# Pair attention in a small transformer kernel: every fourth partition, four chunks of 512 tokens, eight unrolled blocks, keys read in place

## The reference

```
x = x + _L1_attn_ref(_layernorm(x, axis=-1), Wq, Wk, Wv)

b, s, d = x.shape                       # 64, 32, 128; H = 16
Q = (x @ Wq.T).reshape(H, b, s, 8)      # K, V alike
scores = jnp.einsum('hbqd,hbkd->hbqk', Q, K)
atten = jax.nn.softmax(scores, axis=-1)
out = jnp.einsum('hbqk,hbkd->hbqd', atten, V).reshape(b, s, -1)
y = out + x
mu = jnp.mean(y, axis=(1, 2), keepdims=True)
var = jnp.var(y, axis=(1, 2), keepdims=True)
return (y - mu) / jnp.sqrt(var + 1e-5)
```

## Time and profile before

| | us |
|---|---|
| median of three runs | 3089.42 |
| lowest, highest | 3085.68, 3090.41 |
| the profiled execution, its own time | 3081.74 |
| the span of its trace | 3080.0 |

### The profile page before, as it was taken

The page is one execution under the profiler, slowest core; times in us unless marked ns, Lnnn a source line. Parts: engine busy times, 40 slices in busy tenths (PEclk is TensorE's granted clock), DMA queues, the critical chain, the costliest instruction groups (busy, mean ns, idle before and its releaser), DMA issues. The chain is left out here.

```text
span 3080.0 us, 35217 instructions
## 1 busy us (share of the span) xinstructions
PE 2488.2 (81%) x11867; PEld 1402.0 (46%) x11875; DVE 2267.4 (74%) x3046; ACT 1868.9 (61%) x2572; POOL 902.2 (29%) x498
## 2 busy tenths in 40 slices
PE   6699999998899999999999999954366641435998
PEld 3366666663344444444444444322355521423665
DVE  4487777754999999999999999855899921534443
ACT  4365555545888888888888889842455520013443
POOL 1021111111444444444444444300200031102665
PEclk9899999999999999999999999975667775557999
DMA  1000000001000000000000000000011013010000
GB/s 53 11 25 15 18 18 14 14 8 69 1 0 35 1 35 0 34 0 35 0 34 0 35 0 0 0 11 16 10 35 34 21 36 49 5 29 33 16 16 14
DMA packets 17732, 60.16 MB, mean 20 GB/s; under 512 B 1520, under 2 KB 10032, under 8 KB 15664
## 3 DMA queue, kind: packets, MB, share of 16 engines
q1 hardware_dynamic: 17584, 58.29, 6.2%
HBM read 53.04 MB, written 5.24 MB: 19 GB/s over the span
## 5 line engine op out<-in xcount | busy, mean ns | idle before, releaser
L251 PE MATMUL a_ps<-a_x,a_w 128*128 128x512 f32 x1536 | 695.6, 598 | 24.7 <-DVE a_kf L599 12.4
L251 PEld LDWEIGHTS a_ps<-a_x,a_w 128*128 128x128 f32 x1536 | 291.5, 191 | 404.3 <-issue 367.8
L774 POOL TENSOR_TENSOR a_den<-a_qf,a_ksum 128x1024 f32<-128x1024 f32 x128 | 271.2, 2119 | 510.2 <-DVE a_qf L592 473.5
L777 POOL TENSOR_TENSOR a_num<-a_qf,a_kvsum 128x1024 f32<-128x1024 f32 x128 | 295.0, 2304 | 186.1 <-DVE a_kvsum L617 186.0
L2137 DVE TENSOR_REDUCE x_rn<-x_sqk 128x8 f32<-128x512 f32 x256 | 174.3, 681 | 104.8 <-ACT x_sqk L2061 100.6
L2061 ACT ACTIVATE x_sqk<-x_b_k 128x512 f32<-128x512 f32 x256 | 153.1, 598 | 155.8 <-PE x_b_k L1973 149.3
L262 PE MATMUL a_ps<-a_att,a_w 128*128 128x512 f32 x480 | 215.8, 592 | 0.0
L592 DVE SCALAR_TENSOR_TENSOR a_qf<-a_eq,a_qf 128x1024 f32<-128x1024 f32 x128 | 195.4, 1526 | 1.7
L1954 POOL TENSOR_TENSOR x_kn<-x_craw,x_w 128x256 f32<-128x256 f32 x64 | 47.1, 736 | 509.7 <-DVE x_craw L2126 488.1
L445 ACT ACTIVATE a_den<-a_den,consts 128x1024 f32<-128x1024 f32 x128 | 147.0, 1149 | 57.3 <-POOL a_den L774 57.3
L599 DVE SCALAR_TENSOR_TENSOR a_kf<-a_ek,a_ps 128x1024 f32<-128x1024 f32 x128 | 155.5, 1215 | 27.8 <-ACT a_ps L441 23.1
(11 more groups left out here) (417 smaller groups left out, 5480.3 us busy)
## 6 DMA issues: line engine op xcount, KB each, us to landing
a_w<-layers SPq DMA_DIRECT2D x8, 2577.0 KB, 9.2
x_craw<-ctx SPq DMA_DIRECT2D x32, 256.0 KB, 2.6
y_cx<-ctx_t SPq DMA_DIRECT2D x16, 512.0 KB, 3.2
m_w<-experts SPq DMA_DIRECT2D x8, 608.0 KB, 3.8
x_w<-xattn_w SPq DMA_DIRECT2D x1, 2048.0 KB, 7.3
x_all<-x_t SPq DMA_DIRECT2D x1, 1024.0 KB, 4.9
t_scratch<-t_tmp SPq DMA_DIRECT2D x1, 1024.0 KB, 3.9
t_q<-t_scratch SPq DMA_DIRECT2D x4, 256.0 KB
```

The source lines that it names most:

```text
L251: last = nc.tensor.matmul(bank(tile, j), col(par, part * HK + u * P, P), x[:, t0:t0 + BANK], start=True, stop=True)
L774: nc.gpsimd.tensor_tensor(by_batch(den[:, b, :]), by_batch(qf[:, b, :]), bcast(ksum[:, b, :], S), ALU.mult).then_inc(d_ready, 1)
L777: nc.gpsimd.tensor_tensor(by_batch(num[:, b, :]), by_batch(qf[:, b, :]), bcast(kvsum[:, b, :], S), ALU.mult).then_inc(n_ready, 1)
```

## The change

The stage becomes one block of code without barriers inside.

- The layout by heads uses partitions 32g, 32g + 4, ..., 32g + 28 (`ROW_STEP = 4`) instead of 32g to 32g + 7. The zeros between stay, so products read all 32 rows.
- The feature norm is written out in the stage, with ScalarE squaring. q and v are kept by ScalarE, k by VectorE, each in quarters of 512 tokens; a quarter is stored and spread by heads by itself, in an order written out by hand.
- There are 8 blocks of half the size, unrolled, and scores, staged q, turned v and turned probabilities have two buffers. TensorE reads the keys of a pair from `by_head[1]` directly (16 runs of two neighbouring numbers, 2 KB apart), so GpSimd stages only q.
- After every two blocks the outputs of 128 tokens of each quarter (a chunk of 512 tokens) go to DRAM and come back, and the batch norm of the chunk is done among the later blocks. VectorE sums over a batch first, and TensorE then averages 16 sums instead of 512 tokens.

```
@@ -1306,9 +1306,14 @@
 GROUPS = 4
 GTOK = TOK // GROUPS
 PAIR_ROWS = 2 * HEADS
-BLOCKS = 4
+
+
+BLOCKS = 8
 BPAIRS = GTOK // 2 // BLOCKS
 BCOL = BPAIRS * PAIR_ROWS
+ROW_STEP = 4
+CHUNKS = 4
+CTOK = TOK // CHUNKS
...
-            by_head = [sbi(n + "8", [P, HEADS, GTOK]) for n in "qkv"]
-            staged = [sbi(n + "s", [P, BCOL]) for n in "qkv"]
...
-                        for i in range(3):
-                            sp.wait_ge(kept, 2 * i + 2)
-                            sp.dma_start(scratch[i], qkv_t[i][:, :]).then_inc(stored, 16)
-                            sp.wait_ge(stored, 16 * (i + 1))
-                            if i == 0:
-                                sp.wait_ge(cleared, 3)
-                            for g in range(GROUPS):
-                                sp.dma_start(by_head[i][32 * g:32 * g + DH, :, :],
-                                             scratch[i].rearrange("(j c) t -> c j t", c=DH)[:, :, g * GTOK:(g + 1) * GTOK]
-                                             ).then_inc(spread, 16)
...
-                    def _(pool):
-                        for t in by_head:
-                            nc.gpsimd.memset(t[:, :, :], 0.0).then_inc(cleared, 1)
...
-                                r = slice(32 * g, 32 * g + DH)
-                                last = nc.tensor.matmul(psum_s[32 * g:32 * g + 32, c], staged[0][r, c], staged[1][r, c],
-                                                        start=True, stop=True)
-                            last.then_inc(scored, 1)
...
-                        scores(0, True)
-                        with pe.Fori(0, BLOCKS - 1) as i:
-                            scores(i + 1)
-                            outputs(i)
-                        outputs(BLOCKS - 1)
...
-                        with pool.Fori(0, BLOCKS) as i:
-                            pool.wait_ge(s_used, i + 1)
-                            nc.gpsimd.tensor_copy(rows_of(staged[0]), heads_of(by_head[0], i)).then_inc(q_staged, 1)
-                            nc.gpsimd.tensor_copy(rows_of(staged[1]), heads_of(by_head[1], i)).then_inc(k_staged, 1)
...
-                        sp.wait_ge(o_free, BLOCKS + 1)
-                        for g in range(GROUPS):
-                            sp.dma_start(scratch[3].rearrange("(j c) t -> c j t", c=DH)[:, :, g * GTOK:(g + 1) * GTOK],
-                                         o8[32 * g:32 * g + DH, :, :]).then_inc(o_stored, 16)
-                        sp.wait_ge(o_stored, 16 * GROUPS)
-                        sp.dma_start(o_t[:, :], scratch[3]).then_inc(gathered, 16)
-                        sp.wait_ge(gathered, 16)
...
+        q_st = sb("qs", [P, 2, BCOL])
+        v_st = sb("vs", [P, BCOL])
+        v_rows = sb("v_rows", [P, 2, BCOL])
+        prob = sb("prob", [P, BCOL])
+        prob_t = sb("prob_t", [P, 2, BCOL])
+        red = sb("red", [P, BPAIRS])
+        sums = sb("sums", [P, 4, TOK // S])
+        o8, o_t, square = by_head[0], tmp, q_t
...
+        def scores_of(i):
+            return ps[:, i % 2 * BCOL:(i % 2 + 1) * BCOL]
+
+        out_ps = ps[:, 4 * BANK:4 * BANK + BCOL]
+        mean_ps, var_ps = bank(6), bank(7)
...
+        def chunk(ap, c):
+
+            return ap[:, :].rearrange("p (g t) -> p g t", g=GROUPS)[:, :, c * P:(c + 1) * P]
+
+        def packed(ap, c):
+
+            return ap[:, of(c)].rearrange("p (g t) -> p g t", g=GROUPS)
+
+        def rows_in(g):
+            return slice(32 * g, 32 * (g + 1), ROW_STEP)
+
+        def in_scratch(i, g, first, last):
+
+            return scratch[i].rearrange("(j c) t -> c j t", c=DH)[:, :, g * GTOK + first:g * GTOK + last]
...
+                def store(i, p):
+                    sp.wait_ge(kept[i], p + 1)
+                    sp.dma_start(scratch[i][:, of(p)], qkv_t[i][:, of(p)]).then_inc(stored[i][p], 16)
+
+                def by_heads(i, p):
+                    sp.wait_ge(stored[i][p], 16)
+                    sp.wait_ge(cleared, i + 1)
+                    sp.dma_start(by_head[i][rows_in(p), :, :], in_scratch(i, p, 0, GTOK)).then_inc(spread[i], 16)
...
+                store(0, 0)
+                store(0, 1)
+                store(1, 0)
+                by_heads(0, 0)
+                store(0, 2)
+                store(1, 1)
+                by_heads(0, 1)
+                by_heads(1, 0)
+                store(0, 3)
+                store(1, 2)
+                by_heads(0, 2)
+                by_heads(1, 1)
+                store(1, 3)
+                by_heads(0, 3)
+                store(2, 0)
+                by_heads(1, 2)
+                store(2, 1)
+                by_heads(1, 3)
+                store(2, 2)
+                by_heads(2, 0)
+                store(2, 3)
+                for p in range(1, 4):
+                    by_heads(2, p)
...
+                def store_output(first, last):
+                    for g in range(GROUPS):
+                        sp.dma_start(in_scratch(3, g, first, last), o8[rows_in(g), :, first:last]).then_inc(o_stored, 16)
+
+                stores = 0
+                for c in range(CHUNKS):
+                    if c < CHUNKS - 1:
+                        sp.wait_ge(o_kept, 2 * c + 2)
+                        store_output(c * P, (c + 1) * P)
+                        stores += GROUPS
+                    else:
...
+                            sp.wait_ge(o_kept, 2 * c + 1 + h)
+                            store_output(c * P + h * (P // 2), c * P + (h + 1) * (P // 2))
+                            stores += GROUPS
+                    sp.wait_ge(o_stored, 16 * stores)
+                    sp.dma_start(packed(o_t, c), chunk(scratch[3], c)).then_inc(o_loaded[c], 16)
...
+            def _(pool):
+                for t in by_head:
+                    nc.gpsimd.memset(t[:, :, :], 0.0).then_inc(cleared, 1)
+                for i in range(BLOCKS):
+                    if i == 0:
+                        pool.wait_ge(spread[0], 16 * GROUPS)
+                    wait_past(pool, scored, i - 1)
+                    nc.gpsimd.tensor_copy(rows_of(q_st[:, i % 2, :]), heads_of(by_head[0], i)).then_inc(q_staged, 1)
...
+                def scores(i):
+                    pe.wait_ge(q_staged, i + 1)
+                    if i == 0:
+                        pe.wait_ge(spread[1], 16 * GROUPS)
+                    wait_past(pe, shifted, i - 1)
+                    out = scores_of(i)
+                    for g, n in turns():
+                        c = slice(n * PAIR_ROWS, (n + 1) * PAIR_ROWS)
+                        r = slice(32 * g, 32 * g + 32)
+                        t = 2 * (i * BPAIRS + n)
+                        last = nc.tensor.matmul(out[r, c], q_st[r, i % 2, c], by_head[1][r, :, t:t + 2], start=True, stop=True)
+                    last.then_inc(scored, 1)
+
+                def outputs(i):
+                    pe.wait_ge(v_turned, i + 1)
+                    pe.wait_ge(p_turned, i + 1)
+                    wait_past(pe, o_kept, i)
+                    for g, n in turns():
+                        c = slice(n * PAIR_ROWS, (n + 1) * PAIR_ROWS)
+                        r = slice(32 * g, 32 * g + 32)
+                        last = nc.tensor.matmul(out_ps[r, c], v_rows[r, i % 2, c], prob_t[r, i % 2, c], start=True, stop=True)
+                    last.then_inc(attended, 1)
...
+                def batch_mean(c):
+                    pe.wait_ge(y_summed, c + 1)
+                    wait_past(pe, mu_set, c)
+                    nc.tensor.matmul(mean_ps[:, 0:nb], ones, sums[:, 0, c * nb:(c + 1) * nb], start=True, stop=True).then_inc(y_mean, 1)
...
+                scores(0)
+                scores(1)
+                outputs(0)
+                scores(2)
+                outputs(1)
+                scores(3)
+                outputs(2)
+                scores(4)
+                batch_mean(0)
+                outputs(3)
+                scores(5)
+                outputs(4)
+                scores(6)
+                batch_var(0)
+                batch_mean(1)
+                outputs(5)
+                scores(7)
+                outputs(6)
+                outputs(7)
+                batch_var(1)
+                batch_mean(2)
+                batch_var(2)
+                batch_mean(3)
+                batch_var(3)
...
+                for i in (0, 2):
+                    for p in range(4):
+                        keep(i, p)
+                exponentials(0)
+                for i in range(1, 5):
+                    exponentials(i)
+                    keep_output(i - 1)
+                squares(0)
+                exponentials(5)
+                keep_output(4)
+                rstd(0)
...
+                def turn_v(i):
+                    if i == 0:
+                        dve.wait_ge(spread[2], 16 * GROUPS)
+                    wait_past(dve, v_turned, i)
+                    nc.vector.tensor_copy(rows_of(v_st[:, :]), heads_of(by_head[2], i)).then_inc(v_staged, 1)
+                    dve.wait_ge(v_staged, i + 1)
```

(45 more changed lines are left out.)

321 lines of the change are left out of this document (146 added, 175 removed).

## The result

| | before | after |
|---|---|---|
| median, us | 3087.55 (4 runs) | 2968.84 (4 runs) |
| lowest, highest | 3083.45, 3090.41 | 2958.34, 2971.6 |
| profiled execution, its span | 3080.0 | 2966.0 |
| the stage, from its start to its last addition | 284.6 | 163.7 |

The ratio is 0.961, 95% interval 0.9584 to 0.9637: about 119 us less. In the two traces the stage is 120.9 us shorter, the stages ahead of it 1.8 us longer (its start 2493.65 against 2491.86) and the last stage 5.2 us longer. The 2977 predicted lie 8 us above the median.

A forecast was written before the change was run, and what follows sets the result against it. Slow DMA, transfer order and TensorE's instruction arrival bound the stage. Its end moves from 2776.5 to 2662.5 (114), less 2 is 112 off 3081.74, giving 2969.7, plus 7.7 makes 2977 us; range 2952 to 3012.

The forecast's parts named there:

- Start: Stage start: three memsets of 6.93 us run ahead, before each is asked for; first store near 2503.
- Spreads: Transfers into the layout by heads: 100 ns per 2 KB packet, issues 0.35 us, all 288 packets ended at about 2533.
- First block: Scores(0) at 2525; VectorE turns v, then softmax 7.8 us; outputs(0) at 2543.5, TensorE idle 5 us before.
- Blocks: Unrolled loop after outputs(0) starts: 3584 matmuls, 3.7 us per 128, 101 us, end 2646; the branches' 4.57 us each go.
- fetch rule: TensorE's instructions in straight code: next 16 KB fetched mostly hidden, branches break this; rival of closing gaps, 2956, chance 0.13.
- End: Behind the last block: keep, store, reload and norm of the last chunk, 16.5 us instead of 46, ending at 2662.5.
- The 2 us that I took off for a lower clock: Mixture of experts behind the stage: TensorE arrives at the lower clock after longer idle, costing 2 us of the gain.
- the sum of 112: Whole kernel: 114 us from the stage's earlier end, less 2, taken from the profiled execution's 3081.74.
- the 7.7 us added: Whole kernel: median of the runs shown, 3089.42, lies 7.7 us above the profiled execution, raising 2969.7 to 2977.

The follow-up runs named there:

- step 1: Changed kernel with the layout by heads on neighbouring partitions instead of every fourth: median 2998.92 us, ratio to before 0.9697.
- step 2: Changed kernel with the layout by heads on every second partition instead of every fourth: median 2978.19 us, ratio to before 0.9648.
- step 4 alone: Kernel before with only its whole-tensor spreads and store of outputs moved to every fourth partition: 3045.1 us, ratio 0.9852.
- the softmax first: Changed kernel with VectorE taking the softmax of block 0 before the first turning of v: 2969.97 us, ratio to before 0.9631.

## Why the prediction was right

**Start.** The first store was said to come 10.9 us into the stage and came at 10.6; the zeroing of all three tensors at 6.93 us each ran ahead as forecast.

**Spreads.** At 100 ns a packet v was to land 41 us into the stage, and landed at 40.1; the packet measured 82 ns. By the rule of the Trainium skill ("SBUF — State Buffer", DMA port swizzle) it was 75, and v six us earlier; the packet came near that, v did not. The last three spreads of v leave SyncE only from 2524.30 to 2529.28; the prediction had a store's landing at 2.6 us and covered by the stores issued between, and an issue at 0.35 us. The landings took 3.7 to 5.5 us and left SyncE waiting 9.2 us, and an issue took 0.66 to 0.83. So the time of v was right by luck, with two errors that cancel: the packets were cheaper than said, issues and waits dearer. Which of issues and waits weighs more is not tested. Scores(0) was said at 33 us and came at 32.0.

**First block.** v came 1 us earlier and its copy took 0.69 us instead of 1.3, so outputs(0) starts 49.9 us in, not 51.6. TensorE waited 4.27 us before it (5 said).

**Blocks.** 3.59 us a step against 3.7; bursts of 1.93 for scores and outputs; no gap above 2.1 us between 2544 and 2642, but one of 3.17 before, with spreads of v in flight. TensorE ends its last outputs 98.6 us after the first begin, where 102.5 were said. That the gaps stay in straight code is what the kernel with unrolling alone shows, too; the half of the fetch rule of the Trainium skill ("Runtime: NRT & Kernel Launch", instruction fetch) that speaks of a hidden fetch does not hold for these products, the half on a branch does.

**End.** 15.2 us against 16.5: keep 1.1, stores and landing 4.0, reload 2.9, the norm of the last chunk 7.1.

**Around it.** The stage came out at 163.7, said 170.6: 7 us better. The 2 us that I took off for a lower clock behind it were 5.2, with 1.8 ahead of it, and both are as large as the differences between any two kernels here. So the sum of 112 became 114 in the traces: the profiled execution was said to take 2969.7 us and took 2967.8. The 8 us by which the median lies below 2977 are nearly all the 7.7 us added from the profiled execution of before to its median; in the changed kernel that distance is only 1.0.

Where the 120.9 us come from, by the experiments: 69 ahead of the first scores, 19 in the blocks, 33 behind them. The partitions, added to the kernel before, give 33 of the 69 and 13 of the last 33; the branches 11 of the 19; the chunked end another 13 of the last 33. Before the first scores the other 36 come with parts of 512 tokens, early zeroing and one block of code; nothing here separates these. In the blocks some 8 are left, which the two buffers and the double number of blocks would explain (TensorE need not wait for GpSimd's copies), and behind them some 7, where the barriers and the products over all tokens are gone; both are argued, not tested. The shares depend on the order: taken out of the changed kernel, the partitions are worth 35 us (step 1), not the 45 that they give alone.

## What to carry to other kernels

When a transfer shows a DMA share near a half and few GB/s, look at which partitions it touches before changing its size or its order: spreading eight rows over 32 partitions took a 2 KB packet from 267 to 85 ns with nothing else changed, at no cost to the products. For products this small count instructions, not columns or bytes: halving the columns gave nothing, halving the instructions (by bf16 operands) some 27 us. And compare the changed stage in the traces besides the medians, since unchanged code behind it differed by up to 12 us.

## What the hardware showed that I had not expected

- An issue of a spread takes SyncE 0.27 to 0.34 us where eight neighbouring partitions are the target (before, and with step 1) and 0.66 to 0.83 with step 2 or 4. The four whole output stores, 8.06 us to issue in the earlier trace rows, took 3.29 with step 4 alone. The smaller ones of a chunk took 2.68 to 3.54 with step 4 and 2.80 to 2.95 with step 1, so there the step makes no such difference.
- A moving operand in runs of 8 bytes, or 4 in bf16, 2 KB or 1 KB apart costs TensorE what a contiguous one does: 1.93 us per 128 matmuls in float32, and in bf16 0.86 us for 84 against 0.85.
- Zeroing 8192 elements a partition takes GpSimd 6.92 us, in float32 as in bf16.
- The steps of 128 matmuls in straight code have a mean, from outputs(0) to outputs(7), of 3.56 us in the changed kernel, 3.72 in the two with step 2 and with the softmax first, and 3.86 with step 1, though TensorE's list is the same in all four.
- While slow transfers are in flight, the gap between packets of TensorE's instructions grows: 7.84 us with spreads at step 1, 3.18 at step 2 and 3.17 at step 4, against mostly 1.3 to 2.1 otherwise. The traces show that they coincide; the cause is not tested.
